# One RWKV-6 layer with a ternary feed-forward part on one core: cross products in four strips, folded GELU sums, a moved down piece, shared diagonal copies, and tanh values spread by on-chip transfers

## The chip, the cores and the metric

One core of a Trainium2 chip runs one program for the whole layer. The time is the device time of one execution in microseconds (us). Float32 is used throughout, except that the feed-forward products take float16 pairs (a high part and a rest) against ternary weights.

## The reference, cut to what matters

The input is x of 4 sequences x 2048 steps x 512 channels. The layer computes:

- an RWKV-6 time mix with 16 heads of 32 channels: each step is mixed with its predecessor. Five mixing inputs (w, k, v, r, g) come from `tanh((x + xx*maa_x) @ maa_w1)`, which has 5 x 32 = 160 columns, and from a second product of each 32 of these columns with `maa_w2[f]` (32 x 512)
- keys k, values v, queries r and a gate g from 512 x 512 products, and a decay per channel and step, `exp(-exp(w))`
- the recurrence `y = r (S + u k v)`, `S = d S + k v` for every head; a normalisation of y over each head, the gate, an output product, a residual sum and a layer normalisation
- a feed-forward part: a product with ternary weights to 2048 columns, exact GELU, a layer normalisation over the 2048 columns, a product back to 512 columns, a residual sum, a layer normalisation.

## The kernel before, in words

**Tiles and stages.** The 2048 steps are cut into 32 tiles of 64 steps. A tile holds 64 steps of all 4 sequences, so 256 columns; the sequences go in two pairs, p = 0 and 1, of 128 columns. `tile(it, ...)` does the time mix of tile `it`, and between its stages come pieces of the feed-forward part of tile `it - 1` (`ffn.up`, `ffn.down`, `ffn.stats`, `ffn.late` and so on). Tiles 2 to 31 are a loop on each engine; tiles 0 and 1 stand before it, and `alone()` does the last feed-forward part after it. Each engine has its own program, and these are written out by hand; the order of the pieces in each program is the order in which the engine runs them. Semaphores join the engines. The `Ring` objects number the users of the accumulator banks, so that a product waits until the earlier user of its bank has been read.

**The recurrence inside a tile.** Products within a tile of 64 steps are built by levels. The two `l1` products give 32-step blocks; `l2`, `l4`, `l8`, `l16` (L470 to L485) fill in larger distances, each preceded on VectorE by `scale_right` (L1169), `scale_left` (L1180) and a `queries` copy (L1159), and merged by a predicated copy (L1221). `l32` (L490 to L499) gives the cross products between the first and second 32 steps of each sequence. `matrices(p)` on ScalarE (L793 to L809) copies the four diagonal 32 x 32 blocks of each head from A to AB (one instruction for each block of 32 partitions) and then the two cross blocks from the accumulator. For p = 1 the fourth diagonal block is copied by GpSimd (L943). TensorE then does `keys(p)` (L507, transposes), `from_state(p)` (L521) and `from_chunk(p)` (L533); the latter needs all of AB. `outputs(p)` on VectorE (L1233) copies the result out, and `state(h)` (L1241) adds to the state what `values(p)` (L561) made.

**The l32 product before.** A pair's products go to a bank of their own, in 32-column strips that begin at accumulator partitions 0 and 64:

```python
b = 2 * p + h
mm = pe.matmul(psW[64 * h:64 * h + BLK, W.bank(name), 128 * c:128 * (c + 1)],
               cc(KM, c)[:, CH * b:CH * b + BLK], RB[0][:, c, :, BLK * b:BLK * (b + 1)], ...)
```

**GELU sums.** For the layer normalisation over 2048 columns, `add` (L1331, L1334) on VectorE sums GELU values and their squares of four groups into SUMS (2 x 512 per partition). For p = 0 `stats` on TensorE sums over partitions with eight products of one column (L652); for p = 1 VectorE first folds 512 to 128 with two reductions (L1350), and two products are enough (L649). `moments` (L1356 to L1362) makes mean and variance of it, `scale_root` on GpSimd (L912) the inverse root, and `product` (L1369 to L1374) applies them to the down product. `normed` (L1380 to L1385) and `stored` (L1389) follow.

**Tanh values.** `mix_high` on ScalarE writes TMA (128 x 256, four groups of 32 rows) and TMB (32 x 256). It rounds them to TMH and TMBH (L704, L714). Ten more copies (L698, L699) bring the rounded values of each group f to partition groups 0 and 2 of MT[f]. `mix_low` on GpSimd (L905) does ten subtractions that bring the rests to partition groups 1 and 3. `mix(t, f, ...)` on TensorE (L383) waits for both. The first use, `mix(it, 0, "mw")`, stands between the two output products wo0 and wo1 (L611), and `mix(it, 1, "mk")` opens the next tile.

**The start of a tile on TensorE** (L407 to L428): the mk mix; `td1` (L412); `ffn.late()`, which is the last quarter of the down product of pair 1 (L663, 8 products, `down(before, 1, 3)`); the mv mix; `td2` (L424); then the key products (L402). td2's results are exponentiated by ScalarE (L736) before their banks can be used for the keys.

**SyncE** issues all transfers on one queue: XT of the next tile (L304), XTOK (L306), and the two stores (L314).

Of the kernel before, what the change touches and what calls it, by code (L numbers as in the profile page):

```python
# [26 lines left out]
BLK = 32  # L27
# [22 lines left out]
         ("l32_0", "act"), ("l32_1", "act"), ("xt0", "dve"), ("xt1", "dve")]  # L50
# [12 lines left out]
class Ring:  # L63


    def __init__(self, seq, depth, filled, emptied, before={}, banks=None):
# [5 lines left out]
        assert self.n % depth == 0  # L72
# [34 lines left out]
def rwkv_ffn_kernel(nc, x_ch, x_tok, w_all, w1, w2a, w2b, td1, td2, par, wfc, wpj, ffn_wb, c_f32, c_mask, out,  # L107
                    tiles=TILES):
    with ExitStack() as ctx:
# [38 lines left out]
        TMA, TMH = K1[:, 0:COLS], K1[:, COLS:2 * COLS]  # L148
        TMB, TMBH = K1[0:MIXR, 2 * COLS:3 * COLS], K1[0:MIXR, 3 * COLS:4 * COLS]
# [5 lines left out]
        RM = ARENA2[:, 3584:4608]  # L155
        XTOK = KM.rearrange("p (h c) -> p h c", h=PAIRS)
# [39 lines left out]

        W2RAW = (OUT[:, 0:2, :], X1[:, 0:2, :], V[:, 0:1, :])
# [20 lines left out]
        tm_rounded, mt_high, mt_low, w2_split = sem("tm_rounded"), sem("mt_high"), sem("mt_low"), sem("w2_split")  # L218
# [4 lines left out]
        ab_diag, ab_rest = sem("ab_diag"), sem("ab_rest")  # L223
# [13 lines left out]
        W = Ring(W_SEQ, 2, w_full, {"act": w_act, "dve": w_dve})  # L237
# [27 lines left out]
        NWEIGHTS = 8 + 5 * 4  # L265
# [14 lines left out]
        def _(sp):  # L280
# [8 lines left out]
            for dst, src in ((W1[:, :, :], w1), (TD1[:, :, :], td1),  # L289
                             (TD2[0:DECR, :], td2), (TD2[DECR:2 * DECR, :], td2), (WALL[:, W_K, :, :], w_all[:, W_K, :, :])):  # L290
                sp.dma_start(dst, src).then_inc(weights_in, 16)
# [6 lines left out]

            def tile(it, first, ffn):
# [6 lines left out]
                sp.dma_start(XTOK[:, :, :], x_tok[it]).then_inc(xtok_in, 16)  # L306
                if ffn:
# [22 lines left out]
        def _(pe):  # L330
# [39 lines left out]
            pe.wait_ge(xm_ready, 1)  # L370
            tanh_argument("w1a").then_inc(tm_first, 1)
# [19 lines left out]
            def tile(it, first, ffn):  # L391
# [23 lines left out]
                if ffn:  # L415
                    ffn.late()
# [4 lines left out]
                for c in range(KC):  # L421
                    for h in range(2):
# [67 lines left out]
                for p in range(PAIRS):  # L490
                    name = f"l32_{p}"
                    W.wait_free(pe, it, name, first)
                    for c in range(KC):
                        for h in range(2):
                            b = 2 * p + h
                            mm = pe.matmul(psW[64 * h:64 * h + BLK, W.bank(name), 128 * c:128 * (c + 1)],  # L496
                                           cc(KM, c)[:, CH * b:CH * b + BLK], RB[0][:, c, :, BLK * b:BLK * (b + 1)],
                                           start=True, stop=True, skip_group_check=True)
                    mm.then_inc(w_full, 1)  # L499
# [984 lines left out]
```

## Time and profile before

| | |
|---|---|
| three runs | 3108.07, 3111.87, 3113.85 us; median 3111.87 |
| the profiled execution, first to last instruction (span) | 3113.6 us; the trace shows no other time of this execution |
| TensorE busy | 2943.4 us, 95% of the span |
| VectorE busy | 2445.0 us, 79% |
| ScalarE busy | 1976.6 us, 63% |
| GpSimd busy | 894.4 us, 29% |
| granted TensorE clock, mean | 0.991 |
| moved by transfers | 73.40 MB |

PE is TensorE's matmul, PEld its weight load, DVE VectorE, ACT ScalarE, POOL GpSimd, SP SyncE. A float32 matmul of the source shows as two records, so 16 matmuls are "x32". Busy matmul times overlap by a pipelined end. "idle before" is how long the engine stood still ahead of a row, with what ended it.

### The profile page before, as it was taken

Reading aid. Unit: us, or ns where it says so; the run is one execution under the profiler, and the core shown is the slowest. Engines: PE = TensorE matmul, PEld = TensorE weight load, DVE = VectorE, ACT = ScalarE, POOL = GpSimd, SP = SyncE. Lnnn points to the kernel's source line nnn. Section 1 sums busy time; section 2 is a strip of 40 time slices with the busy share of each in tenths; the row PEclk is TensorE's granted clock in tenths of the full one; section 3 lists DMA queues with packets and bytes.
Section 4 is the critical chain, followed back from the end, with each engine's and each line's share of the span. In section 5 each row is a group of like instructions: output and inputs, shape, how many; then the busy total and the mean of one; then the engine's idle time right before and its main releaser. Section 6 shows DMA issues by size and latency. Waiting matters only on the chain.

```text
span 3113.6 us, 102428 instructions
## 1 busy us (share of the span) xinstructions
PE 2943.4 (95%) x40633; PEld 2187.3 (70%) x40633; DVE 2445.0 (79%) x5275; ACT 1976.6 (63%) x4175; POOL 894.4 (29%) x790
## 2 busy tenths in 40 slices
PE   1889999999999999999999999999999999999997
PEld 0667777777777777677777777777777777777775
DVE  8467887787887787787778787778788778788777
ACT  0456676666677666677666667666667666667764
POOL 1223221333222233322233322233322233322222
PEclk9899999999999999999999999999999999999998
DMA  5000000000000000000000000000000000000000
GB/s 212 8 15 22 13 23 19 22 15 22 12 23 19 22 15 22 16 19 19 22 15 22 22 12 19 22 17 21 22 12 23 19 22 15 22 12 23 19 22 14
DMA packets 22823, 73.40 MB, mean 24 GB/s; under 512 B 3105, under 2 KB 3361, under 8 KB 20769
## 3 DMA queue, kind: packets, MB, share of 16 engines
q1 hardware_dynamic: 22432, 67.10, 6.3%
q8 instruction: 379, 6.21, 0.8%
q14 instruction: 12, 0.09, 0.0%
HBM read 50.31 MB, written 16.78 MB: 22 GB/s over the span
## 4 chain that ended last, share of the span: by engine, by line
PE 70%; DVE 19%; issue 6%; ACT 3%; DMA 1%; DVEq 1%; SPq 0%; ACTq 0%; POOLq 0%; POOL 0%
PE psP L402 18%; PE psF L636 11%; PE psP L440 7%; PE psP L611 7%; PE psF L663 6%; DVE HLO L1342 4%; PE psW L479 2%; PE psY L533 2%; PE psY L521 2%; DVE SUMS L1334 2%; PE psW L496 2%; PE psF L652 2%; DVE ARENA L1091 2%; DVE ARENA L1169 1%; DVE ARENA L1279 1%
## 5 line engine op out<-in xcount | busy, mean ns | idle before, releaser
L402 PE MATMUL psP<-ARENA,WALL 128*128 128x256 f32 x3072 | 698.7, 383 | 39.4 <-ACT ARENA L736 39.4
L693 ACT ACTIVATE ARENA<-ARENA 32x512 f32<-32x512 f32 (+3 forms) x1026 | 584.4, 570 | 221.2 <-DVE ARENA L1169 92.4
L402 PEld LDWEIGHTS psP<-ARENA,WALL 128*128 128x128 f32 x3072 | 573.7, 191 | 117.5 <-ACT ARENA L736 42.4
L1342 DVE SCALAR_TENSOR_TENSOR HLO<-GG,FWB,HHI 128x128 f16<-128x128 f32 x1024 | 347.6, 400 | 321.4 <-ACT HHI L864 316.3
L636 PE MATMUL psF<-XHI,WFC 128*128 128x128 f16 x4096 | 488.5, 220 | 1.9 <-DVE ST L1356 1.9
L636 PE MATMUL psF<-XLO,WFC 128*128 128x128 f16 x4096 | 487.1, 220 | 0.0
L905 POOL TENSOR_TENSOR MT<-ARENA 32x256 fp32r<-32x256 f32 x330 | 318.5, 965 | 467.3 <-ACT ARENA L693 438.7
L919 POOL TENSOR_TENSOR ARENA<-ARENA,XT 128x1024 f32<-128x1024 f32 x128 | 278.7, 2178 | 533.9 <-DVE ARENA L1103 533.9
L636 PEld LDWEIGHTS psF<-XHI,WFC 128*128 128x128 f16 x4096 | 398.3, 98 | 37.7 <-issue 32.9
L636 PEld LDWEIGHTS psF<-XLO,WFC 128*128 128x128 f16 x4096 | 402.0, 98 | 17.9 <-issue 10.3
L663 PE MATMUL psF<-WPJ,HHI 128*128 128x512 f16 x1024 | 390.9, 382 | 14.4 <-ACT GG L855 14.4
L663 PE MATMUL psF<-WPJ,HLO 128*128 128x512 f16 x1024 | 389.2, 380 | 0.0
L864 ACT ACTIVATE HHI<-GG,FWB 128x128 f16<-128x128 f32 x1024 | 327.3, 390 | 25.4
L912 POOL TENSOR_TENSOR FV<-FV,CF 128x1 f32<-128x1 f32 x64 | 35.1, 549 | 965.7 <-DVE FV L1362 965.7
L855 ACT ACTIVATE GG<-psF 128x512 f32<-128x512 f32 x256 | 150.8, 589 | 197.2 <-PE psP L402 136.0
L611 PE MATMUL psP<-WALL,ARENA 128*128 128x512 f32 x512 | 233.5, 599 | 4.6 <-DVE ARENA L1282 2.8
L440 PE MATMUL psP<-WALL,ARENA 128*128 128x512 f32 x512 | 224.9, 592 | 0.0
L693 ACT ACTIVATE ARENA<-psP 128x256 f32<-128x256 f32 (+1 forms) x192 | 93.8, 528 | 162.6 <-PE psP L402 162.6
L663 PEld LDWEIGHTS psF<-WPJ,HHI 128*128 128x128 f16 x1024 | 99.8, 97 | 131.2 <-issue 25.1
L855 ACT ACT_TABLE_LOAD x62 | 79.5, 1283 | 157.3 <-PE psP L440 153.1
L1103 DVE SCALAR_TENSOR_TENSOR ARENA<-psX,PAR,XX 128x256 f32<-128x256 f32 x324 | 140.7, 475 | 40.9 <-PE psX L383 40.9
L479 PEld LDWEIGHTS psW<-ARENA 128*32 128x32 f32 x8192 | 122.3, 110 | 69.6 <-issue 69.6
(165 smaller groups left out, 5242.1 us busy)
## 6 DMA issues: line engine op xcount, KB each, us to landing
XT<-x_ch SPq DMA_DIRECT2D x33, 520.0 KB, 3.4
ARENA<-x_tok SPq DMA_DIRECT2D x32, 512.0 KB, 3.5
out<-OUT SPq DMA_DIRECT2D x64, 256.0 KB, 2.1
WALL<-w_all SPq DMA_DIRECT2D x5, 1024.0 KB, 15.3
ARENA<-wfc SPq DMA_DIRECT2D x4, 1024.0 KB, 8.0
ARENA<-wpj SPq DMA_DIRECT2D x3, 1024.0 KB, 14.7
GG<-wpj SPq DMA_DIRECT2D x1, 1024.0 KB, 18.7
OUT<-w2a SPq DMA_DIRECT2D x8, 64.0 KB, 14.0
```

Source lines behind the costliest of these rows:

```text
L402: mm = pe.matmul(psP[:, P.bank(f"{name}{g}"), COLS * c:COLS * (c + 1)], WALL[:, w, k, 128 * (2 * g + c):128 * (2 * g + c + 1)], cc(XF[slot ...
L440: mm = pe.matmul(psP[:, P.bank(f"v{p}"), :], cc(XF[1], k)[:, 128 * p:128 * (p + 1)], WALL[:, W_V, k, :], start=(k == 0), stop=(k == KC - 1))
L479: mm = pe.matmul(psW[BLK * (q % 4):BLK * (q % 4 + 1), W.bank(name), o:o + 64], cc(KM, c)[:, BLK * q:BLK * (q + 1)], RB[RB_SEQ[name]][:, c, ...
L611: mm = pe.matmul(psP[:, P.bank(f"wo{p}"), :], cc(YSB, k)[:, 128 * p:128 * (p + 1)], WALL[:, W_O, k, :], start=(k == 0), stop=(k == KC - 1))
L636: mm = pe.matmul(psF[:, F.bank(name), 128 * m:128 * (m + 1)], WFC[:, k, 128 * (4 * g + m):128 * (4 * g + m + 1)], x[:, p, k, :], start=(k ...
L663: mm = pe.matmul(psF[:, F.bank(f"pj_{p}"), :], h[:, m, :], WPJ[:, m, :], start=(m == 0 and h is HHI), stop=(m == MH - 1 and h is HLO))
L693: return act.activation(o, i, ACT.Copy)
L855: act.activation(GG[:, u % 2, 0, :], psF[:, F.bank(f"fc{g}_{p}"), :], ACT.Gelu).then_inc(f_act, 1)
L864: e = act.activation(HHI[:, k, :], GG[:, u % 2, 0, 128 * m:128 * (m + 1)], ACT.Copy, scale=FWB[:, 0, k:k + 1])
L905: pool.tensor_tensor(MT[f][rows(1 + 2 * (n % 2)), :], whole, high, ALU.subtract).then_inc(mt_low, 1)
L919: pool.tensor_tensor(v, v, xcur, ALU.add).then_inc(xf_ready, 1)
L1342: e = dve.scalar_tensor_tensor(out=HLO[:, k, :], in0=GG[:, u % 2, 0, 128 * m:128 * (m + 1)], scalar=FWB[:, 0, k:k + 1], in1=HHI[:, k, :], ...
```

## The change

1. **Cross products in four strips**: l32 is one stage for both pairs in one bank. The strip begins at partition 64h + 32p, and the order is c, p, h; the bank order of the W ring is written out. ScalarE's cross copies read the new place.
2. **Folded GELU sums**: `fold` is two tensor additions in place of two reductions, and is done for both pairs; `stats` is always two products. Its place on TensorE moves from behind l32 to behind `from_chunk(0)`.
3. **Moved down piece**: `ffn.late()` moves on TensorE from behind td1 to behind td2.
4. **Shared diagonal copies**: of the diagonal blocks, ScalarE copies 0 and 1 for each pair, VectorE copies 2 and 3 for pair 0 and 2 for pair 1; GpSimd keeps its one.
5. **Tanh values spread by transfers**: the columns of W1 are reordered at the start (one GpSimd copy), so that TMA's partition 4e + f holds row e of group f. ScalarE only rounds, GpSimd only subtracts (one instruction for TMA, one for TMB), and SyncE issues eight SBUF to SBUF transfers a tile: four of 128 KB for groups 0 to 3, four of 32 KB for group 4. TMBH and TMBL lie in RM.
6. **Order**: on TensorE `from_state(0)` goes ahead of `keys(0)`, and `ffn.up(1, 0)` goes behind `from_state(1)`. On VectorE the two feed-forward pieces `moments` and `product` are parted, and `normed` goes behind `outputs(1)`.

```diff
+W_BANKS = [0, 1, 0, 1, 0, 1, 0, 1, 0]
...
+            def spread(t):
+
+                sp.wait_ge(tm_rounded, 2 * t + 3)
+                for copy in (0, 2):
+                    sp.dma_start(MT32[rows(copy), 0:4, :], TMH).then_inc(mt_first, 16)
+                sp.wait_ge(tm_rest, 2 * t + 3)
+                for copy in (1, 3):
+                    sp.dma_start(MT32[rows(copy), 0:4, :], TML).then_inc(mt_first, 16)
+                sp.wait_ge(tm_rounded, 2 * t + 4)
+                for copy in (0, 2):
+                    sp.dma_start(MT32[rows(copy), 4, :], TMBH).then_inc(mt_last, 16)
+                sp.wait_ge(tm_rest, 2 * t + 4)
+                for copy in (1, 3):
+                    sp.dma_start(MT32[rows(copy), 4, :], TMBL).then_inc(mt_last, 16)
...
                 sp.dma_start(XTOK[:, :, :], x_tok[it]).then_inc(xtok_in, 16)
+                spread(it)
...
-                pe.wait_ge(mt_high, 5 * (t + 1) + f + 1)
-                pe.wait_ge(mt_low, 10 * (t + 1) + 2 * f + 2)
+                pe.wait_ge(mt_first if f < 4 else mt_last, 16 * 4 * (t + 2))
...
-                if ffn:
-                    ffn.late()
                 mix(it - 1, 2, "mv", wait_free)
...
+                if ffn:
+                    ffn.late()
                 channels("k", W_K, 1, 0, (0,))
...
-                for p in range(PAIRS):
-                    name = f"l32_{p}"
-                    W.wait_free(pe, it, name, first)
-                    for c in range(KC):
+                W.wait_free(pe, it, "l32", first)
+                for c in range(KC):
+                    for p in range(PAIRS):
                         for h in range(2):
-                            b = 2 * p + h
-                            mm = pe.matmul(psW[64 * h:64 * h + BLK, W.bank(name), 128 * c:128 * (c + 1)],
+                            b, o = 2 * p + h, 64 * h + BLK * p
+                            mm = pe.matmul(psW[o:o + BLK, W.bank("l32"), 128 * c:128 * (c + 1)],
...
-                if ffn:
-                    ffn.stats(0)
...
+                from_state(0)
                 pe.wait_ge(m_dve, M.read(it, "mg1"))
                 pe.wait_ge(k_scaled, NPL * it + 6)
                 keys(0)
...
-                from_state(0)
                 from_chunk(0)
+                if ffn:
+                    ffn.stats(0)
                 keys(1)
+                from_state(1)
                 if ffn:
                     ffn.up(1, 0)
-                from_state(1)
                 from_chunk(1)
...
-                    for q in range(3 if p else 4):
+                    for q in range(2):
...
-            def mix_low(t, start, end):
+            def mix_low(t):
...
+                pool.tensor_tensor(TML.bitcast(F32R), TMA, TMH, ALU.subtract).then_inc(tm_rest, 1)
+                pool.wait_ge(tm_rounded, 2 * t + 4)
+                pool.tensor_tensor(TMBL.bitcast(F32R), TMB, TMBH, ALU.subtract).then_inc(tm_rest, 1)
...
+                diagonal(0, (2, 3))
                 scale_left(5, 32)
                 if ffn:
-                    ffn.finish()
+                    ffn.fold()
...
                 outputs(0)
+                diagonal(1, (2,))
+                if ffn:
+                    ffn.stats()
                 dve.wait_ge(m_dve, M.read(it, "mg1"))
                 differences(it + 1)
                 if ffn:
+                    ffn.finish()
+                outputs(1)
+                if ffn:
                     ffn.normed()
-                outputs(1)
...
-                def fold(j, p, i):
+                def fold(j, p):
                     dve.wait_ge(sums_added, 3 * (PAIRS * j + p) + 3)
-                    dve.tensor_reduce(GR[:, i, :], SUMS[:, i, :].rearrange("p (m t) -> p t m", m=4), AX.X, ALU.add).then_inc(sums_folded, 1)
+                    dve.tensor_tensor(SUMS[:, :, 0:256], SUMS[:, :, 0:256], SUMS[:, :, 256:512], ALU.add).then_inc(sums_folded, 1)
+                    dve.wait_ge(sums_folded, 2 * (PAIRS * j + p) + 1)
+                    dve.tensor_tensor(GR[:, :, :], SUMS[:, :, 0:128], SUMS[:, :, 128:256], ALU.add).then_inc(sums_folded, 1)
```

In the changed VectorE program `ffn.stats()` is `moments(j, 0)` and `ffn.finish()` is `product(j, 0)`; `diagonal(p, strips)` makes one copy of 32 partitions x 512 for each strip.

## Rows read from the trace of the kernel before

**Rows 1.** The page's first line.

```profile
span 3113.6 us, 102428 instructions
```

**Rows 2.** Windows, one tile: stretch, us, busy us (instructions) by engine, clock, DMA share, GB/s.

```profile
1517.20:1609.80 92.60, 90.61 (x1270) 67.49 (x1274) 74.02 (x164) 61.62 (x132) 27.32 (x24) 1.00 0.06 19
```

**Rows 3.** Waits of PE: us in total, times, longest.

```profile
PE psP L402 <- ACT ARENA L736: 39.4, 32, 1.4
...
PE psW L479 <- DVE ARENA L1180: 17.7, 33, 2.1
```

**Rows 4.** PE in order of time, one tile: start us, us, line, operands, records.

```profile
1517.12 1.96 PE L462 MATMUL psW<-ARENA 128*32 128x128 f32 x64
...
1536.37 1.94 PE L496 MATMUL psW<-ARENA 128*32 128x128 f32 x32
1538.24 1.95 PE L652 MATMUL psF<-CF,SUMS 128*128 128x1 f32 x16
1540.05 0.64 PE L507 MATMUL psX<-CF,ARENA 128*128 128x128 f32 x4
1540.62 1.10 PE L521 MATMUL psY<-ARENA 32*32 32x64 f32 x64
1541.64 1.08 PE L533 MATMUL psY<-ARENA,V 128*32 128x128 f32 x32
```

**Rows 5.** DVE in order of time, the same tile.

```profile
1538.36 0.69 DVE L1180 TENSOR_TENSOR ARENA<-ARENA,TOT 128x512 f32<-128x512 f32 x1 [1.67 <-PE psW L496]
1540.23 0.16 DVE L1356 TENSOR_SCALAR ST<-psF 128x2 f32<-128x2 f32 x1 [1.18 <-PE psF L652]
...
1542.65 1.27 DVE L1228 SCALAR_TENSOR_TENSOR ARENA<-ARENA,psP 128x512 f32<-128x512 f32 x2
...
1547.20 0.69 DVE L1233 COPY ARENA<-psY 128x512 f32<-128x512 f32 x1 [0.54 <-PE psY L533]
...
1552.27 0.42 DVE L1241 TENSOR_TENSOR ARENA<-ARENA,psX 128x256 f32<-128x256 f32 x1 [0.46 <-PE psX L561]
```

**Rows 6.** ACT in order of time, the same tile.

```profile
1536.72 2.55 ACT L693 ACTIVATE ARENA<-ARENA 32x512 f32<-32x512 f32 x4 [2.08 <-DVE ARENA L1221]
1539.29 1.19 ACT L693 ACTIVATE ARENA<-psW 32x512 f32<-32x512 f32 x2
```

**Rows 7.** DVE by line and form: count, busy us, mean ns.

```profile
L1159 DVE COPY ARENA<-ARENA 32x512 f32<-32x512 f32 x160 | 67.8, 424 | 12.3 <-PE psW L462 8.1
```

**Rows 8.** POOL in order of time, the same tile.

```profile
1541.15 0.55 POOL L912 TENSOR_TENSOR FV<-FV,CF 128x1 f32<-128x1 f32 x1 [29.98 <-DVE FV L1362]
1542.92 1.27 POOL L943 TENSOR_TENSOR ARENA<-ARENA,CF 32x512 f32<-32x512 f32 x1 [1.23 <-PE psY L533]
...
1562.51 1.85 POOL L905 TENSOR_TENSOR MT<-ARENA 32x256 fp32r<-32x256 f32 x2 [13.71 <-ACT ARENA L693]
```

**Rows 9.** The chain that ended last, same tile: start us, us, what.

```profile
1534.59 1.83 PE psF L663 x8
...
1543.31 1.79 PE psF L636 x32
```

**Rows 10.** PE in order of time, around the tile's change.

```profile
1563.84 3.70 PE L611 MATMUL psP<-WALL,ARENA 128*128 128x512 f32 x8
...
1571.94 1.09 PE L412 MATMUL psP<-ARENA,TD 128*64 128x128 f32 x16
...
1575.28 1.16 PE L424 MATMUL psP<-TZ,TD 64*128 64x128 f32 x16
```

**Rows 11.** DVE in order of time, the same stretch.

```profile
1573.30 0.68 DVE L1291 TENSOR_TENSOR X<-psP,ARENA 128x512 f32<-128x512 f32 x1
```

**Rows 12.** DMA issues: KB each, median us to landing.

```profile
XT<-x_ch SPq DMA_DIRECT2D x33, 520.0 KB, 3.4
...
out<-OUT SPq DMA_DIRECT2D x64, 256.0 KB, 2.1
...
OUT<-w2a SPq DMA_DIRECT2D x8, 64.0 KB, 14.0
```

More of the change, by code:

```diff
@@ L514, in from_state @@
                         pe.wait_ge(y_copied, 2 * it + 1)
-                    elif not first:
-                        pe.wait_ge(x_dve, X.read(it - 1, "kv1"))
                     for c in range(KC):
@@ L529, in from_chunk @@
                         pe.wait_ge(ab_rest, it + 1)
-                    pe.wait_ge(w_act, W.read(it, f"l32_{p}"))
+                    pe.wait_ge(ab_dve, 2 * it + p + 1)
+                    if p:
+                        pe.wait_ge(w_act, W.read(it, "l32"))
+                    else:
+                        pe.wait_ge(ab_cross, it + 1)
                     for c in range(KC):
@@ L710, in mix_high @@
                 e.then_inc(tm_ready, 1)
-                for f in range(1, 4):
-                    high(t, f)
                 act.wait_ge(tm_ready, M.read(t, "w1b"))
-                copy(TMBH.bitcast(F32R), TMB[:, :]).then_inc(tm_rounded, 1)
-                high(t, 4)
+                copy(TMBH.bitcast(F32R), TMB).then_inc(tm_rounded, 1)
             act.wait_ge(su_dve, 6)
@@ L765, in tile @@
                     if not first:
-                        act.wait_ge(w_full, W.full(it - 1, "l32_1" if p == 0 else "l16"))
+                        act.wait_ge(w_full, W.full(it - 1, "l32" if p == 0 else "l16"))
                     for h in range(HPG):
@@ L1180, in scale_left, with diagonal @@
                     dve.tensor_tensor(left, left, grow(tr, n), ALU.mult).then_inc(k_scaled, 1)
+                def diagonal(p, strips):
+                    for q in strips:
+                        r = slice(BLK * q, BLK * (q + 1))
+                        e = dve.tensor_copy(AB[r, :, BLK * q:BLK * (q + 1)],
+                                            A[r, 512 * p:512 * (p + 1)].rearrange("p (h t) -> p h t", h=HEADS))
+                    e.then_inc(ab_dve, 1)
                 dve.wait_ge(p_act, P.read(it, "r1"))
@@ L1184, in tile @@
                     if not first:
-                        dve.wait_ge(w_full, W.full(it - 1, "l32_1" if p == 0 else "l16"))
+                        dve.wait_ge(w_full, W.full(it - 1, "l32" if p == 0 else "l16"))
                     for h in range(HPG):
@@ L1326, in add @@
                     if g == 1:
-                        if p:
-                            dve.wait_ge(f_full, F.full(j, "st_0"))
-                        elif not first:
-                            dve.wait_ge(sums_folded, 2 * j)
+                        if p or not first:
+                            dve.wait_ge(sums_folded, 2 * (PAIRS * j + p))
                         e = dve.tensor_tensor(SUMS[:, :, :], GG[:, 0, :, :], GG[:, 1, :, :], ALU.add)
@@ L1401, in late_fold @@
                     if not first:
[L1402 to L1403 removed]
+                        fold(before, 1)
                 def alone():
@@ L1421, in alone @@
                         stored(j, p)
-                return FeedForward(normalise=normalise, tokens=tokens, up=up, finish=lambda: finish(j, 0), normed=lambda: normed(j, 0),
+                return FeedForward(normalise=normalise, tokens=tokens, up=up, fold=lambda: fold(j, 0), stats=lambda: moments(j, 0), finish=lambda: product(j, 0), normed=lambda: normed(j, 0),
                                    stored=lambda: stored(j, 0), late_fold=late_fold, moments=lambda: late(moments), late=lambda: late(product), late_normed=lambda: late(normed), late_stored=lambda: late(stored), alone=alone)
```

89 lines of the change are left out of this document (36 added, 53 removed).

## Prediction

> **What bounds the kernel now.** I read the page first: the span is 3113.6 us [rows 1]. That is 1.7 us above the median of the three runs, 3111.87, so the sum is made against 3113.6 and 1.7 is taken off at the end. The parts of the chain that ended last repeat every 92.6 us, so one tile is enough, and the windows view of it comes next: TensorE (PE) is busy 90.61 of 92.60 us, VectorE (DVE) 74.02 [rows 2]. PE's waits say where the other 2 us are: 39.4 us in 32 times ahead of the first key product, which waits for ScalarE's exponentials, and 17.7 us ahead of the level products, which wait for VectorE [rows 3]. So PE is nearly full, and taking work from it can pay. But the chain passes to DVE in two stretches (from l1 to l32, and from the state update to the output product), and there a faster PE only waits. So the gain has to be found stage by stage. Times below are those of that tile less 1500.
>
> **Part 1, the strips.** l1 runs 64 records in four strips in 1.96 us; l32 runs 32 records in two strips at a time and takes 1.94 [rows 4]. Same shapes, so in four strips I take 0.98: l32 runs from 36.37 to 37.35, 0.9 us less of PE.
>
> **Part 2, the sums.** stats(0) is 16 records from 38.24 to 40.05, 1.81 us [rows 4]; four records cost 0.45, so 1.36 us less of PE. VectorE pays a fold for pair 0: a 128x512 addition like L1180, 0.69, and one of half that size like L1241, 0.42, together 1.1 us [rows 5].
>
> **Walk through the strip stage, with parts 4 and 6.**
> - from_state(0) now follows l32 at once: 1.02 us (40.62 to 41.64 [rows 4]), until 38.4.
> - keys(0) waits for scale_left. VectorE's last predicated copy ends at 36.7 (ScalarE starts then [rows 6]); two diagonal copies like L1159 cost 0.42 each [rows 7], scale_left 0.69: 38.25. No wait; keys(0) takes 0.57 (40.05 to 40.62 [rows 4]), until 38.95. Copies of 32x512 on VectorE can't be under 0.42 by this row nor over ScalarE's 0.64; I take 0.42, since it is the same engine and size.
> - from_chunk(0) waits for ScalarE: two diagonal copies, half of 2.55, then the cross copies, 1.19 [rows 6]: 39.2. So PE idles 0.35 and runs from 39.3 to 40.35.
> - stats(0) until 40.8 (the fold is done at 39.4), keys(1) until 41.35.
> - from_state(1) waits for outputs(0). VectorE: fold until 39.4, two gates 1.27 until 40.65 [rows 5], copy 0.69 until 41.35. So from_state(1) runs from 41.45 to 42.5: the piece that hid this wait, up(1, 0), has moved behind it, and almost nothing is left to hide.
> - up(1, 0) takes 1.79 [rows 9], until 44.3. Its bank needs the first small operation of moments, at 42.0 (diagonal copy 0.42 after outputs(0)).
> - from_chunk(1) needs GpSimd's diagonal copy, and GpSimd's order puts the inverse root ahead of it. moments lasts 0.92 (40.23 in [rows 5] to 41.15 in [rows 8]), so until 42.7; root 0.55, copy 1.27 [rows 8], with the two handovers 44.8. PE idles 0.5 and ends at 45.95. Before, that GpSimd copy was done at 44.2, early enough; it is the new last wait.
> - VectorE until then: product is 1.5 (40.23 to 42.65 less 0.92), differences and normed together at most 2.05 (43.92 to 47.20 less a copy and 0.54 idle [rows 5]); it is free by 46.0.
>
> outputs(1) thus starts at about 46.05 instead of 47.20 [rows 5]: **1.15 us gained** of 2.26 taken from PE. normed now follows outputs(1); VectorE still idled 0.46 ahead of L1241 [rows 5], waiting for PE, and more ahead of its first HLO piece, so I cost it at nothing; without that cover it would be 0.6 us. From there to the output product the chain is VectorE's and nothing in it changes.
>
> The Trainium skill (TensorEngine Tiling (Array Packing), Key Properties) says that changing the tiling mode drains TensorE, and the new order of l32, state, keys, chunk, stats and up has eight such changes where the old one had seven. The rows bound it: from_chunk's 32 records take 1.08 alone, and half of l1's take 0.98 [rows 4], so a change costs at most 0.1 us, 3 us in all if the rule shows fully. I leave it inside the range.
>
> **Part 5, tanh values.** Ten 32x256 copies leave ScalarE and eight subtractions GpSimd (two cost 1.85 [rows 8]), all beside PE's output products and of no price on the path. What comes in is a transfer ahead of mix "mw". The rounding copy ends at about 62.4 (GpSimd starts at 62.51 [rows 8]). One 128x256 subtraction I bound by 0.93 (half of 1.85) and 1.27 (L943); 1.0 taken: 63.5. The last of the four first transfers is issued by 64.0 (an estimate, one issue behind the other). Landing after issue: 2.1 us for 256 KB, 3.4 for 520 KB [rows 12]; each is 128 KB but four run together, so 2.4 taken, ends 2.1 and 3.4: 66.1 to 67.4. The mix comes at 63.84 + 3.70 = 67.5 [rows 10]. Hidden, with 0.1 to 1.4 us to spare. Behind the mix stand wo1 and td1, so every us too late would be a us of the tile. The SP queue: eight more issues, all between XTOK and the store, which waits for work 10 us later; XT's load comes later still. K1 may be overwritten only after mt_last, 15 us on.
>
> The skill's page SBUF — State Buffer, on the port swizzle, gives 189 GB/s for writes to partitions 0..31, and DMA: Bandwidth & Descriptors a fixed 2.0 us; 256 KB to each half of the ports makes an estimate of 3.4 us, the upper end of my rows. By it the slack is gone but the sum unchanged.
>
> **Part 3, the down piece.** From td1's end, 73.03, PE spent 2.25 on the down piece and the mv mix, 1.16 on td2 [rows 10] and 1.22 waiting [rows 3]: key product at 77.66. Now the mix comes first; td2 then waits for its bank, which VectorE reads until 73.98 [rows 11]: 74.05 to 75.2. The down piece takes 1.83 [rows 9], until 77.05. The exponentials needed 1.22 after td2, so 76.45: hidden. **0.6 us gained.** The stretch from there to l1 is PE's own and unchanged; VectorE's faster fold of pair 1 is off the path.
>
> **The sum.** 1.75 us in each of 31 tiles is 54; the first tile has no feed-forward pieces and gives about 0.9; the closing feed-forward part saves 2 (the smaller stats and folds). The set-up's one GpSimd copy for W1 and its transfers stand beside other work: 0, between -3 and +3. 3113.6 - 57 - 1.7 = 3055.
>
> **The rivals.**
> - **Fuller.** The waits of 0.35 and 0.5 that I put in PE's way aren't there (ScalarE or GpSimd sooner). For it: each hangs on a sum of four or five durations. Against: they are rows. 2.6 us a tile: 3113.6 - 81 - 3 = 3030. PE's work and its key wait together, 3.5 a tile, are the limit: 3005.
> - **Partly given back.** The transfers land up to 0.5 us late, or normed isn't covered: 1.1 us a tile, 3113.6 - 34 - 3 = 3076.
> - **The strips don't overlap**, because their order is 0, 64, 32, 96. l32 ends at 38.24, from_chunk(0) starts at 39.85: 0.55 of the 1.15 is lost; 1.2 a tile, 3073. Against: l1.
> - **Slower: the transfers are late by several us**, ahead of mix "mw". The slack is 3.5 from issue; with 1.75 gained, it decides from 5.3 us of landing on. For it: 64 KB transfers into 32-partition pieces took 14.0 [rows 12]. Against: those stood in a queue behind megabytes. At 7 us: 3.5 - 1.75 = 1.75 lost, 3113.6 + 54 = 3168; at 5.8 us 3129.
> - **Nothing changes**: the late chains to the output product eat all of it; only if VectorE, not PE, set outputs(1). The 0.54 idle there [rows 5] is against it.
>
> **How the numbers follow.** Forecast 0.57 (3045 to 3066 for itself), fuller 0.13, partly given back 0.13, strips 0.06, slower 0.06, nothing 0.05. About 0.2%, 6 us, is what a measurement of this kernel can tell from no change. Faster 0.89, same 0.05, slower 0.06. The range 3026 to 3084 takes in the fuller and the lesser cases and leaves out slower, nothing and the far end of fuller.
>
> **What would show it.** l32's row at about 1.0 us for 32 records; the 512 records of L652 gone from PE's groups; from_chunk(1) ended by a wait for GpSimd's L943; PE's wait ahead of the key product gone and a small one ahead of td2; no wait ahead of mix "mw". A tile of 90.85 us. Wrong would be a PE wait ahead of that mix for MT or a DMA, a td2 that waits over 1 us, or a tile under 90.2 or over 91.6.

## The result and the profile after

The changed kernel takes 3093.26 us, the median of four runs (3091.97 to 3095.24), beside 3112.86 us for the kernel before on the same chip (3108.07 to 3114.17). The ratio is 0.9944, with an interval of 0.993 to 0.9959. It is faster by 20 us by the medians, by 17 by the ratio, where I forecast 57, and its time lies above my range. The direction was right and the size was wrong by two thirds.

The page of the kernel after, first lines; they answer to [rows 1] and the table:

```profile
span 3093.4 us, 101000 instructions
...
PE 2904.9 (94%) x40249; PEld 2115.8 (68%) x40249; DVE 2453.0 (79%) x5435; ACT 1794.1 (58%) x3749; POOL 664.7 (21%) x527
```

Windows of one tile of the kernel after, with the columns of [rows 2]:

```profile
1513.79:1605.98 92.19, 89.50 (x1256) 65.26 (x1255) 74.20 (x169) 55.96 (x118) 20.28 (x16) 1.00 0.09 26
```

The work did leave the engines. PE has 1.1 us a tile less, ScalarE 5.7, GpSimd 7.0. The tile became only 0.44 us shorter on the mean: from the start of the first l1 product to the end of the last, divided by 31, it is 92.63 before and 92.19 after. (Start to start it is 0.06 less, in every kernel.) PE stands still for 2.69 us of this tile where it stood still for 1.99 [rows 2]. So PE's waits tell the story. Waits of PE after, in us, times, longest:

```profile
PE psY L561 <- issue: 43.0, 31, 1.5
...
PE psX L408 <- DMA MT<-ARENA: 4.5, 26, 0.2
...
PE psP L427 <- ACT ARENA L746: 2.7, 2, 1.4
```

The key products' wait of 39.4 us [rows 3] is gone (L402 is now L427). In its place stands one of 43.0 us ahead of the second `from_chunk` (L561), and a small one for the transfers that bring the tanh values (L408). To see what each is worth I measured one tile in stretches, from one PE group's start to the next one's, as a mean over the 27 tiles 3 to 29:

| stretch, us | before | after | forecast change | change |
|---|---|---|---|---|
| l1 to l32 | 19.26 | 19.50 | 0 | +0.24 |
| l32 to second `from_chunk` | 9.68 | 9.31 | -1.15 | -0.37 |
| from there to the variance products | 6.17 | 6.18 | 0 | +0.01 |
| from there to the first output product wo0 | 11.61 | 11.62 | 0 | +0.01 |
| wo0 to td1 | 8.13 | 8.64 | 0 | +0.51 |
| td1 to the first key product | 5.71 | 5.02 | -0.6 | -0.69 |
| first key product to l1 | 32.08 | 31.97 | 0 | -0.11 |
| sum | 92.64 | 92.23 | -1.75 | -0.41 |

The sum misses the forecast by 1.34 us a tile: 0.78 ahead of the second `from_chunk`, 0.51 ahead of td1 and 0.24 ahead of l32, with 0.2 better than forecast behind td1. For the whole, 31 tiles by 0.44 are 13.6 us; the set-up and the first tile give 0.9 (l1 first runs at 129.1 instead of 130.0), and what lies behind the last l1 gives 5.7, together 20.2: the spans' difference.

**The strip stage after.** PE of the kernel after in order of time, with the columns of [rows 4], in the tile of the windows row above:

```profile
1528.18 1.08 PE L524 MATMUL psW<-ARENA 128*32 128x128 f32 x32 [0.24 <-issue]
1529.19 1.09 PE L545 MATMUL psY<-ARENA 32*32 32x64 f32 x64
1530.22 0.66 PE L533 MATMUL psX<-CF,ARENA 128*128 128x128 f32 x4
1530.85 1.08 PE L561 MATMUL psY<-ARENA,V 128*32 128x128 f32 x32
1531.86 0.60 PE L673 MATMUL psF<-CF,GR 128*128 128x1 f32 x4
1532.33 0.64 PE L533 MATMUL psX<-CF,ARENA 128*128 128x128 f32 x4
1533.02 1.20 PE L545 MATMUL psY<-ARENA 32*32 32x64 f32 x64
...
1537.48 1.08 PE L561 MATMUL psY<-ARENA,V 128*32 128x128 f32 x32 [1.37 <-issue]
```

Read against my walk, all goes to plan within 0.3 us up to `from_state(1)` and up(1, 0), which ends at 1536.1, 7.9 us behind l32's start as forecast. (The wait of 0.35 us that I had put ahead of `from_chunk(0)` is not there.) l32 takes 1.08 for 32 records instead of 1.94 [rows 4], stats 0.60 for four records. Then PE waits 1.37 us where I had put 0.5. "issue" means that no releaser shows; `from_chunk` needs all of AB, and the last block comes from GpSimd. POOL in order of time, the same stretch:

```profile
1534.28 1.60 POOL L918 TENSOR_TENSOR FV<-FV,CF 128x1 f32<-128x1 f32 x1 [31.62 <-DVE FV L1381]
1536.12 1.26 POOL L949 TENSOR_TENSOR ARENA<-ARENA,CF 32x512 f32<-32x512 f32 x1 [0.24 <-POOL FV L918]
```

DVE in order of time, the same stretch:

```profile
1534.05 0.15 DVE L1381 TENSOR_SCALAR FV<-ST 128x1 f32<-128x1 f32 x1
1534.25 1.23 DVE L1090 TENSOR_TENSOR XX<-XT 128x1024 f32<-128x1024 f32 x1
...
1538.62 0.69 DVE L1247 COPY ARENA<-psY 128x512 f32<-128x512 f32 x1 [1.58 <-PE psY L561]
```

The inverse root (L918) takes 1.60 us, not the 0.55 of [rows 8]: VectorE's `differences` (L1090, two SBUF inputs, 128x1024) had started 0.03 us ahead of it. The block copy (L949) ends at 1537.38 and PE goes on 0.1 later. The last of ScalarE's cross copies for this pair had ended at 1534.47, so it is GpSimd that PE waits for. In the kernel before, VectorE ran this beside the root of [rows 8], an operation with one SBUF input and one in the accumulator (DVE in order of time):

```profile
1541.02 0.76 DVE L1369 SCALAR_TENSOR_TENSOR psF<-WSUM,ST,psF 128x512 f32<-128x512 f32 x1
```

**The tanh values after.** PE in order of time, from the first output product to the first key product:

```profile
1555.28 3.70 PE L639 MATMUL psP<-WALL,ARENA 128*128 128x512 f32 x8
1559.15 0.49 PE L408 MATMUL psX<-MT,W2S 128*128 128x256 f32 x2 [0.18 <-DMA MT<-ARENA]
...
1563.91 1.09 PE L437 MATMUL psP<-ARENA,TD 128*64 128x128 f32 x16
...
1566.10 1.16 PE L447 MATMUL psP<-TZ,TD 64*128 64x128 f32 x16
1567.19 0.39 PE L683 MATMUL psF<-WPJ,HHI 128*128 128x512 f16 x1
...
1568.93 3.62 PE L427 MATMUL psP<-ARENA,WALL 128*128 128x256 f32 x16
```

SP's queue in order of time, ahead of it:

```profile
1553.90 1.27 SPq L310 DMA_DIRECT2D MT<-ARENA  x2
1555.21 1.25 SPq L313 DMA_DIRECT2D MT<-ARENA  x2
```

The chain that ended last, the same stretch (start us, us, what):

```profile
1555.21 0.60 SPq L313
1555.86 3.17 DMA MT<-ARENA
1559.03 0.12 issue
1559.15 0.49 PE psX L408 x2
```

One issue takes SP 0.60 to 0.63 us, so the fourth begins at 1555.86 and lands 3.17 us later, at 1559.03. That is 5.1 us after the first issue began, and the mix can't start before. In the kernel before, this mix started 3.13 us behind wo0's start, ahead of the modelled end of wo0 (PE in order of time; wo0 is the row 1563.84 of [rows 10]):

```profile
1566.97 0.80 PE L383 MATMUL psX<-MT,W2S 128*128 128x256 f32 x2
```

The last lines of PE's rows of the kernel after are part 3: td2 follows td1 by 2.19 us, the down piece hides the exponentials, and the key product starts without a wait.

### The profile page after: what moved, and what is told of

Same layout as the page of the kernel before. It is cut to its first block, busy times and chain, and to the rows that moved or that the text cites. A ratio compares the mean times of both kernels' runs of the same rounds, so it can differ in the third digit from the quotient of the medians.

```text
span 3093.4 us, 101000 instructions
## 1 busy us (share of the span) xinstructions
PE 2904.9 (94%) x40249; PEld 2115.8 (68%) x40249; DVE 2453.0 (79%) x5435; ACT 1794.1 (58%) x3749; POOL 664.7 (21%) x527
## 4 chain that ended last, share of the span: by engine, by line
PE 62%; DVE 18%; issue 8%; ACT 6%; DMA 4%; SPq 2%; DVEq 1%; ACTq 0%; POOLq 0%; POOL 0%
PE psP L427 18%; PE psF L664 11%; PE psP L465 7%; PE psF L683 5%; PE psP L639 4%; DMA MT<-ARENA 3%; DVE HLO L1359 3%; ACT HHI L874 2%; PE psY L561 2%; PE psY L545 2%; DVE SUMS L1351 2%; DVE ARENA L1234 2%; PE psW L504 2%; PE psX L408 2%; DVE ARENA L1096 2%
## 5 line engine op out<-in xcount | busy, mean ns | idle before, releaser
L427 PE MATMUL psP<-ARENA,WALL 128*128 128x256 f32 x3072 | 695.6, 381 | 2.7 <-ACT ARENA L746 2.7
L713 ACT ACTIVATE ARENA<-ARENA 32x512 f32<-32x512 f32 (+3 forms) x930 | 524.2, 564 | 186.7 <-DVE ARENA L1174 90.2
L427 PEld LDWEIGHTS psP<-ARENA,WALL 128*128 128x128 f32 x3072 | 575.8, 191 | 79.8 <-issue 1.8
L1359 DVE SCALAR_TENSOR_TENSOR HLO<-GG,FWB,HHI 128x128 f16<-128x128 f32 x1024 | 317.3, 371 | 283.1 <-ACT HHI L874 278.1
L918 POOL TENSOR_TENSOR FV<-FV,CF 128x1 f32<-128x1 f32 x64 | 67.8, 1060 | 1007.9 <-DVE FV L1381 1007.9
L736 ACT ACTIVATE TZ<-psP 128x128 f32<-128x128 f32 x32 | 8.9, 278 | 323.1 <-PE psP L437 323.1
```

The costliest lines, as they stand in the source:

```text
L427: mm = pe.matmul(psP[:, P.bank(f"{name}{g}"), COLS * c:COLS * (c + 1)], WALL[:, w, k, 128 * (2 * g + c):128 * (2 * g + c + 1)], cc(XF[slot ...
L713: return act.activation(o, i, ACT.Copy)
L1359: e = dve.scalar_tensor_tensor(out=HLO[:, k, :], in0=GG[:, u % 2, 0, 128 * m:128 * (m + 1)], scalar=FWB[:, 0, k:k + 1], in1=HHI[:, k, :], ...
```

## The experiments

Every experiment starts from the kernel after unless it says otherwise. Line numbers move a little between them. A single run of a kernel lies up to 5 us from its median (8 us in e4), so beside the medians I use the tile (first to last l1, over 31) and the stretches of the table. These come from one traced execution of each kernel. The ratios are to runs of the kernel before beside them; the kernel after has 0.9944.

**e1_product_first: the inverse root without its neighbour.** The piece `product` goes ahead of `differences`, so that VectorE does other work while GpSimd takes the root.

```diff
                 if ffn:
                     ffn.stats()
+                if ffn:
+                    ffn.finish()
                 dve.wait_ge(m_dve, M.read(it, "mg1"))
                 differences(it + 1)
-                if ffn:
-                    ffn.finish()
                 outputs(1)
```

> Changed kernel with VectorE's product(j, 0) ahead of differences(it + 1). Theory A (GpSimd's inverse root, which took 1.60 us beside the 1.23 us of differences, is held up by that instruction): the root falls back to 0.55 us, PE's wait ahead of the second from_chunk falls from 1.37 to about 0.3 us, the tile from 92.2 to about 91.3 us, the whole to about 3065 us. Rival B (the root is slow for a cause of its own, or from_chunk(1) waits for something else): the root stays near 1.6 us, the wait near 1.37, the whole within 5 us of 3093.

Measured: 3069.68 us, ratio 0.9874 (0.9855 to 0.9893); the tile is 91.34. POOL of e1 in order of time:

```profile
1520.55 0.55 POOL L918 TENSOR_TENSOR FV<-FV,CF 128x1 f32<-128x1 f32 x1 [31.60 <-DVE FV L1381]
1521.34 1.27 POOL L949 TENSOR_TENSOR ARENA<-ARENA,CF 32x512 f32<-32x512 f32 x1 [0.24 <-POOL FV L918]
```

DVE of e1, the `differences`:

```profile
1522.05 1.64 DVE L1090 TENSOR_TENSOR XX<-XT 128x1024 f32<-128x1024 f32 x1
```

Waits of PE in e1:

```profile
PE psY L561 <- issue: 10.9, 31, 0.5
```

The root is back at 0.55, in every tile, and PE's wait fell from 43.0 to 10.9 us. l32 to the second `from_chunk` is 8.26 (9.31 after), and 0.27 of that is given back behind it (6.45 instead of 6.18). So this one order on VectorE had eaten 0.85 us a tile by the two traces, 26 us; by the medians it is 24 us, by the ratios 22. Now `differences` is the one that is held up: it takes 1.64 beside the block copy instead of 1.23, on an engine that has slack there.

**e2_block_first: GpSimd's block copy ahead of the root.** The other way to mend it.

```diff
                 if ffn:
                     ffn.bias()
-                    ffn.finish()
...
                 pool.wait_ge(ab_rest, it + 1)
+                if ffn:
+                    ffn.finish()
                 pool.wait_ge(tot_ready, NPL * it + 6)
```

> Changed kernel with GpSimd's copy of the last diagonal block ahead of its inverse root instead of behind it; differences still goes ahead of product, so the root stays slow. If GpSimd's order is what makes the copy the last wait of from_chunk(1), that wait of 1.37 us is gone (the copy is done by 33.3 on the clock of the tile shown, the two ScalarE copies by 34.5, up(1, 0) by 36.1), outputs(1) comes 1.3 us sooner, and the whole is about 3055 us; product waits for the slow root but outputs(1) hides it. If from_chunk(1) waits for ScalarE or VectorE in truth, no change: 3093 us.

Measured: 3070.84 us, ratio 0.9878 (0.9861 to 0.9896); the tile is 91.49. That is short of the 3055 expected. It is the same gain as e1, though PE's wait at L561 is gone altogether and the stretch to it is 7.86. POOL of e2 in order of time:

```profile
1518.78 1.61 POOL L918 TENSOR_TENSOR FV<-FV,CF 128x1 f32<-128x1 f32 x1 [1.24 <-DVE FV L1387]
```

Waits of PE in e2:

```profile
PE psF L664 <- DVE OUT L1399: 11.6, 32, 0.5
```

The root still takes 1.61, so `product`, which needs it, is late, and with it the bank that up(1, 1) wants: the next stretch grows from 6.18 to 7.01. What was won ahead of the second `from_chunk` was lost behind it.

**e3_two_queues: half of the transfers issued by ScalarE.** If it is the issue time that makes the transfers late, two queues should help; if the transfers share a limit, they should not.

```diff
-                sp.wait_ge(tm_rounded, 2 * t + 3)
-                for copy in (0, 2):
-                    sp.dma_start(MT32[rows(copy), 0:4, :], TMH).then_inc(mt_first, 16)
...
+                act.wait_ge(tm_rounded, 2 * t + 3)
+                for part in (0, 2):
+                    act.dma_start(MTALL[:, :, :].bitcast(F32)[rows(part), 0:4, :], TMH).then_inc(mt_first, 16)
```

> Changed kernel with the two transfers of TMH issued by ScalarE, so that SyncE issues the two of TML first. Theory C (four issues of 0.6 us one behind another on one queue make the last transfer land 0.3 us too late for mix mw, and the start of the tile loses 0.6 us by it): the last landing comes 0.5 to 1 us sooner after the rounding copy, no wait ahead of mix mw, wo's start to the key product 13.2 instead of 13.8 us, the whole about 3075 us. Rival D (the transfers share a limit of their own, or ScalarE's later steps now set the start of the tile): 3093 us or more.

Measured: 3089.73 us, ratio 0.9933 (0.9916 to 0.9949), the tile 92.10: not to be told from the kernel after. DMA issues of e3, with the columns of [rows 12]:

```profile
MT<-ARENA ACTq DMA_DIRECT2D x66, 128.0 KB, 2.9
MT<-ARENA SPq DMA_DIRECT2D x66, 128.0 KB, 3.6
```

ScalarE's queue of e3 in order of time:

```profile
1552.46 1.21 ACTq L718 DMA_DIRECT2D MT<-ARENA  x2
```

PE of e3, the mix behind wo0 in the same tile:

```profile
1557.67 0.50 PE L405 MATMUL psX<-MT,W2S 128*128 128x256 f32 x2
```

The transfers that SP issues land 3.6 us after issue now instead of 3.1, and the mix starts 5.2 us after the first issue as before. The issues overlap, the landings don't get earlier. By the landing times in the traces (medians over 33 tiles), the fourth issue begins 1.48 us behind the first here and 1.96 in the kernel after. The last landing comes 5.07 and 5.13 us behind the first issue, and in both the four landings follow each other by 0.80, 0.80 and 0.65 us. So the transfers hold each other up, whoever issues them, and it is not the issue time that makes them late. What they share was not tried.

**e4_down_back: part 3 undone.** `ffn.late()` goes back to its place behind td1.

```diff
                 mm.then_inc(p_full, 1)
+                if ffn:
+                    ffn.late()
                 mix(it - 1, 2, "mv", wait_free)
...
-                if ffn:
-                    ffn.late()
                 channels("k", W_K, 1, 0, (0,))
```

> Changed kernel with the down piece back behind td1. If the moved piece does hide ScalarE's exponentials (PE's wait of 1.22 us ahead of the key product was really removed) and the late transfers alone ate that gain, putting it back costs about 0.6 us a tile: 3093 + 19 = 3112 us, with the wait of 1.2 us back. If the move is worth nothing, because td2 waits for its bank in its place, the whole stays within 5 us of 3093.

Measured: 3117.49 us, ratio 1.0024 (1.0014 to 1.0034), the tile 93.10. Part 3 is worth 0.91 us a tile by the two traces, 0.80 by the ratios (the traced execution is the slowest of ten, 8 us above the median), and 0.81 in the two stretches behind td1. Without it the other five parts together make the kernel slower than before. Waits of PE in e4, where the old one is back:

```profile
PE psP L427 <- ACT ARENA L746: 39.5, 32, 1.4
```

**e5_tanh_by_engines: part 5 undone.** ScalarE's ten copies and GpSimd's ten subtractions come back, and the eight transfers go.

```diff
-                spread(it)
...
-                pe.wait_ge(mt_first if f < 4 else mt_last, 16 * 4 * (t + 2))
+                pe.wait_ge(mt_high, 5 * (t + 1) + f + 1)
+                pe.wait_ge(mt_low, 10 * (t + 1) + 2 * f + 2)
...
-                mix_low(it)
+                mix_low(it, 0, 10)
```

> Changed kernel with part 5 undone: MT is filled by ScalarE's copies and GpSimd's subtractions as before. Theory C: the late transfers cost the start of the tile 0.6 us, so from wo's start to the key product it is 13.2 instead of 13.8 us and the whole 3093 - 19 = 3074 us. If something else in the start of the tile ate the moved down piece's gain, the stretch stays 13.8 and the whole is 3093 us or, with the extra work on GpSimd and ScalarE, above.

Measured: 3079.64 us, ratio 0.9895 (0.9879 to 0.9912), the tile 91.92. wo0 to td1 is 8.50, hardly less than 8.64, and td1 to the key product 4.92 (5.02). Waits of PE in e5:

```profile
PE psP L419 <- DVE ARENA L1116: 13.1, 31, 0.8
```

Each subtraction takes GpSimd as long as before (eight in 7.74 us, 0.97 each; two in 1.85 [rows 8]). What is longer is VectorE's row beside them, ahead of the sums that td1 waits for. DVE in order of time, of e5 and of the kernel before:

```profile
1549.56 3.21 DVE L1356 SCALAR_TENSOR_TENSOR HLO<-GG,FWB,HHI 128x128 f16<-128x128 f32 x4
```

```profile
1563.71 2.59 DVE L1342 SCALAR_TENSOR_TENSOR HLO<-GG,FWB,HHI 128x128 f16<-128x128 f32 x4
```

The same four take 1.60 in the kernel after and 1.14 with nothing beside them. So the old way was not free either in the new order, and undoing part 5 gives back only a part of what it costs: 14 us by the medians, where 19 were expected.

**e6_tanh_sooner: the same transfers, started earlier.** ScalarE makes the first tanh and its rounding ahead of the last up piece's GELU instead of behind it.

```diff
                     ffn.up(1, 2)
-                    ffn.up(1, 3)
...
                 act.activation(TMA[:, :], M_BANKS[M.bank("w1a")][:, 0:COLS], ACT.Tanh).then_inc(tm_ready, 1)
+                round_first(it)
+                if ffn:
+                    ffn.up(1, 3)
```

> Changed kernel with ScalarE's first tanh and its rounding ahead of up(1, 3) instead of behind it, so that the transfers start about 2.4 us sooner. Theory C: no wait for them is left, start of wo to key product 13.2 us, whole about 3074 us, the same as without the transfers. Rival: the later up(1, 3) on ScalarE (by 0.8 us) delays VectorE's chain to the output product or the next use of the sums, and the gain is given back: 3093 us.

Measured: 3072.17 us, ratio 0.9871 (0.9854 to 0.9887), the tile 91.50. SP's queue of e6 in order of time:

```profile
1541.04 1.27 SPq L310 DMA_DIRECT2D MT<-ARENA  x2
```

PE of e6 in order of time, the same tile:

```profile
1544.79 3.70 PE L639 MATMUL psP<-WALL,ARENA 128*128 128x512 f32 x8
1547.93 0.80 PE L408 MATMUL psX<-MT,W2S 128*128 128x256 f32 x2
```

The first issue is now 3.75 us ahead of wo0 instead of 1.38, wo0 to td1 is 8.11, as before the change, and td1 to the key product 4.92. So the lateness had cost 0.5 and 0.1 us a tile, and 0.69 with what else moved: 21 us. It was the time that the transfers take against their slack, and not their presence. (The subtraction ahead of the third issue takes 1.58 us here instead of 0.72, beside a VectorE operation of 128x1024 with two SBUF inputs, so the fourth issue begins 2.25 us behind the first; the last landing still comes at 5.16.)

**c126_all_three and c16_no_block_move: the mends together.** c16 is e1 with e6; c126 is e1, e2 and e6.

> Changed kernel with product ahead of differences, GpSimd's block copy ahead of its root, and the sooner tanh, all three. If the causes are separate, the gains add: 3093 - 24 (product first) - 10 (block copy not waited for) - 19 (transfers hidden) = 3040 us. If VectorE's chain to the output product takes over first, as little as 3050 to 3055 us.

> Version with product first and the sooner tanh, but GpSimd's root ahead of its block copy. It tells what moving the block copy is worth once the root takes 0.55 us: PE waited 0.33 us there and starts again more slowly after a wait, so 0.4 to 0.6 us a tile, 3044 + 15 = 3059 us; if the next wait (product behind a later root) eats that, 3044 us.

Measured: c126 3044.48 us, ratio 0.9786 (0.977 to 0.9802), the tile 90.59; c16 3047.30 us, ratio 0.9801 (0.9784 to 0.9817), the tile 90.63. The two can't be told apart, so e2's edit adds nothing that shows to e1's. c126 has the lowest time that I measured, 49 us under the kernel after by the ratios. POOL of c126 in order of time:

```profile
1505.92 1.27 POOL L953 TENSOR_TENSOR ARENA<-ARENA,CF 32x512 f32<-32x512 f32 x1 [29.43 <-PE psY L561]
1508.42 0.55 POOL L923 TENSOR_TENSOR FV<-FV,CF 128x1 f32<-128x1 f32 x1 [1.24 <-DVE FV L1392]
```

Waits of PE in c126:

```profile
PE psF L664 <- issue: 11.2, 14, 1.2
```

The block copy is early, the root short, and the wait ahead of the second `from_chunk` is gone (7.84 from l32). What is left is behind it, ahead of up(1, 1): 6.67 us to the variance products.

**c125_engines: e1, e2 and part 5 undone.** It asks what the transfers are worth once they are hidden.

> As the version with all three mends, but with MT filled by ScalarE and GpSimd as before in place of the transfers and the sooner tanh. If hidden transfers are worth no more than the ten copies and ten subtractions they replace, the same 3044 us. The version on the changed kernel alone was 7 us slower than the sooner tanh, so I expect 3052 us.

Measured: 3056.56 us, ratio 0.982 (0.9803 to 0.9836), the tile 91.20. Beside c126, 90.59: hidden transfers are worth 0.6 us a tile over the engines' copies, 0.38 of it in wo0 to td1 (8.49 and 8.11) and 0.22 behind the second `from_chunk` (6.89 and 6.67).

**b3, b1 and b13: single parts put into the kernel before.** b3 moves the down piece alone (the opposite of e4's edit), b1 makes l32 in four strips alone, b13 does both. b1's core:

```diff
-                for p in range(PAIRS):
-                    name = f"l32_{p}"
-                    W.wait_free(pe, it, name, first)
-                    for c in range(KC):
+                W.wait_free(pe, it, "l32", first)
+                for c in range(KC):
+                    for p in range(PAIRS):
                         for h in range(2):
-                            b = 2 * p + h
+                            b, o = 2 * p + h, 64 * h + BLK * p
```

> Kernel before with part 3 alone: the down piece behind td2. My step says 0.6 us a tile: 3109 - 18 = 3091 us, with the wait of 1.2 us ahead of the key product gone and one of 0.3 to 0.4 us ahead of td2. If the piece hid something where it stood (the wait for the mv or td2 bank in full), the whole stays at 3109 us.

> Kernel before with part 1 alone: l32 for both pairs in four strips. In the order of before PE has no wait between l32 and the second from_chunk, so the 0.9 us that l32 gets shorter should reach outputs(1) in full and the whole be 3112 - 28 = 3084 us. If VectorE or ScalarE take over (scale_left behind l32, ScalarE's cross copies), less than half of it: 3098 us or above.

> Kernel before with parts 1 and 3. The down piece alone gave 28 us. If the two lie on different stretches of the tile they add: 3112 - 28 - 28 = 3056 us, below the whole change at 3093, so that parts 2, 4, 5 and 6 together lose some 37 us. If they share a cover: 3070 to 3084 us.

Measured: b3 3083.69 us, ratio 0.9914 (0.9897 to 0.993), the tile 91.73; b1 3091.33 us, ratio 0.9937 (0.992 to 0.9953), the tile 91.93; b13 3065.82 us, ratio 0.9857 (0.984 to 0.9873), the tile 91.21. The two parts nearly add up (0.90 and 0.70 a tile, together 1.42), and these two alone beat the whole change by 27 us. b3 gains more than the 18 us expected; b1 gains 20 of 28 and b13 45 of 56, and why a part of the strips' gain is missing was not followed up. In b3, td1 to the key product falls from 5.71 to 4.92, as in e6 (5.02 in the kernel after, with its late transfers), and the next stretch from 32.08 to 31.97. In b1, l32 to the second `from_chunk` falls from 9.68 to 9.05, and l1 to l32 stays (19.26). Parts 2, 4 and 6 were not run by themselves.

## Why the prediction was wrong

**The step that failed first: the inverse root's duration in the walk through the strip stage.** I wrote "root 0.55, copy 1.27" and took 0.55 from a row in which VectorE ran something else. The change itself put `differences` in front of `product`, so the root now runs beside a 128x1024 operation with two SBUF inputs and takes 1.60. That is the term that was mis-sized, by 1.05 us: PE waits 1.37 us ahead of `from_chunk(1)` where I had put 0.5, and e1, which mends it, gives back 0.85 us a tile. I had seen that GpSimd's copy was "the new last wait", so nothing covered it. The order was in the diff, and I costed VectorE's two pieces only as a sum of their times, not for who runs beside them.

The Trainium skill (SBUF — State Buffer, Who interferes with whom) says that a VectorE instruction with two SBUF inputs contends with a GpSimd instruction that reads SBUF, and that the one that issues first keeps the shared port pair for its whole length. The trace agrees in both directions: 0.55 became 1.60 behind `differences` and the root ended 0.40 us behind it, and in e1 `differences` went from 1.23 to 1.64 behind GpSimd's copy, which had 0.56 us left when it started. I did not weigh it in the prediction, and it speaks against this order.

**The step that failed second: the last landing and the start of the mix in part 5.** From the end of the rounding copy I had 1.6 us to the last issue, 2.4 to its landing (between 2.1 and 3.4 [rows 12]) and 5.1 until the mix wants it: 1.1 us to spare. In the kernel after, the rounding copy ends 1.40 us ahead of wo0. The last issue then begins 1.98 us behind the copy, each issue taking 0.60 to 0.63, and landing takes 3.17. Which of the two is longer makes no difference: with the last issue 0.5 us sooner (e3) it landed as late. What I had wrong is the time from the first issue to the last landing, 4.0 in my sum and 5.1 measured, because I took one transfer's landing for that of four. And the mix wants it sooner: I had added wo0's full duration, 3.70, but when nothing holds it the mix starts 3.14 us behind wo0's start (e6). The trace of the kernel before had this row already (3.13). So the slack is 1.1 less 0.4, 0.8 and 0.56: -0.6, with 0.1 more from landing to PE. The mix does start 3.87 behind wo0 instead of 3.14, of which 0.2 is won back until td1. The profile's wait of 4.5 us in 26 times tells of far less than the 0.53 a tile that it costs (8.64 less 8.11), because it counts only what lies beyond wo0's modelled end. It is my rival "partly given back", with 0.5 us late, in that half; its other half, `normed` without cover, didn't come (+0.01 to the variance products and as much to wo0).

For the landing, the estimate of 3.4 us that I had made from the Trainium skill (SBUF — State Buffer, on the port swizzle, with the fixed 2.0 us of DMA: Bandwidth & Descriptors) was nearer to the 3.17 of this chain than my 2.4, but by luck: it was meant for all four running together, and from the first issue they took 5.1. Taken for the sum it would have brought the slack to 0.1 us.

**Part 3 was right in kind and too small.** I forecast 0.6, it is worth 0.90 (b3) or 0.8 to 0.9 (e4). Of the 0.3 that I missed, 0.2 is that groups of matmuls follow each other closer than their durations say (td2's 1.16 takes 1.09 to the next start, the down piece's 1.83 takes 1.74), and 0.1 is that the key product runs slower behind a wait: in [rows 3] a wait of 1.2 us stood ahead of it, and l1 came 0.11 later for it.

**The strips were right.** l32 at 1.08 for 32 records, 1.01 to the next group's start (0.98 forecast), stats at 0.60, 0.47 to the next start (0.45), VectorE's fold and diagonal copies at 0.42 to 0.69 as taken. The rival that the four strips don't overlap is out. b1 alone gives 0.70 us a tile of the 0.9 that I took from PE. The one more change of tiling mode costs nothing that shows: `from_state` and `from_chunk` keep their 1.08 to 1.10 in the new order, but for the second `from_state` with 1.20.

**Was the sum sound?** With both failed steps mended, c16 has a tile of 90.63 and c126 of 90.59; I forecast 90.85. So the walk holds to 0.3 us a tile once the root has its 0.55 and the transfers are hidden. Some of that is luck: in c16 part 3 gives 0.3 more than forecast and the strip stage 0.3 more, while l1 to l32 loses 0.24 and the stretch behind the second `from_chunk` 0.25. That last one, which I had called unchanged, grows by 0.3 in e1 and by 0.8 in e2. (The sums of four rivals, 3030, 3076, 3073 and 3168, leave out the 1.7 us that I took off the forecast; nothing hangs on it.)

**What stays open.** l1 to l32 grew by 0.24 us a tile, in e1 to c126 too, and not in b1. PE now waits, ahead of l32, for three semaphores that it used to take later (the scaled queries, the last value bank and the state's reads). The trace narrows it down. From the start of the last down product to l32's start it is 0.32 us with four waits (before, b1, b13) and 0.56 with seven (after), which is the whole growth. In the tile shown none of the work waited for ends later than 1527.56, and the last down product ends at 1527.94. So the number of waits is the likely cause, and not late work; moving these waits behind l32 was not tried. The part behind the last l1 gave 5.7 us where I had 2. The last section says where 2.9 of it come from, and why they can't be credited to the change.

## What to carry to other kernels

A duration taken from the trace belongs to its neighbours: when a change moves a GpSimd operation, ask which VectorE operation will run beside it, and cost it from a row with that neighbour or bound it by one. Transfers that must land ahead of a full engine are costed from the first issue to the last landing of a group like them, not by one transfer's landing, and their lateness counts more than the wait that the profile shows, because the engine loses its overlap as well. When several parts go in together, try the safe ones alone first: here two parts of six gave more than all six, until the other parts' two faults were mended (c16).

## What the runs showed of the hardware that I had not expected

- A GpSimd operation on 128x1 took 0.55 us or 1.60, by which VectorE operation ran beside it (e1 and the kernel after; 1.61 in e2).
- An SBUF to SBUF issue of 128 KB occupied its queue for 0.55 to 0.69 us on SP and ScalarE alike, an ordinary load 0.33 to 0.37. Four of 128 KB into 32 partitions each took 5.0 to 5.2 us from the first issue to the last landing, with one queue or with two (e3) and with the last issue anywhere from 1.5 to 2.3 us behind the first (e3, after, e6).
- The granted clock had a hand in the closing part. In both kernels it fell to the lower level (1.2 GHz) once behind the last tile (6.8 us, from 3060.3 before and from 3045.8 after). In the kernel before it fell again for two groups of PE's products, and in the kernel after it stayed up, though PE was as busy in the 8 us ahead of the down products (5.03 us before, 5.06 after). Windows of the kernel before in the closing part, with the columns of [rows 2], for the down products of pair 0 and the up products behind them:

```profile
3076.00:3085.00 9.00, 8.62 (x33) 3.71 (x34) 4.55 (x10) 4.31 (x12) 0.00 (x0) 0.81 0.01 3
...
3087.00:3091.00 4.00, 3.84 (x41) 3.87 (x42) 3.24 (x11) 0.60 (x1) 0.97 (x2) 0.58 0.00 0
```

The same windows of the kernel after:

```profile
3061.00:3068.00 7.00, 6.91 (x32) 3.06 (x32) 5.61 (x12) 4.06 (x11) 0.00 (x0) 1.00 0.00 1
3068.00:3071.00 3.00, 2.66 (x37) 2.32 (x36) 2.16 (x8) 0.00 (x0) 0.55 (x1) 1.00 0.03 5
```

The same 32 down products take 8.76 us before and 7.07 after in the chain that ended last, the 32 up products 3.20 and 1.96: 2.9 us of the closing part, at a granted share of 0.81 and 0.58 (partly at the lower level, 1.2 GHz) against 1.00. This is no merit of the change: in e3, e4 and e6, whose closing part is that of the kernel after, the same down products take 8.75 us at 0.81, and in e1, e5 and c16 7.07 at 1.00. What decides it was not tried, and these 2.9 us of the 20 can't be counted as the change's.
